# A two-layer attention kernel: the order of the work in which the first layer's loop runs out, and where its norms are split and shifted

## The reference

```python
# first layer, per batch: cross attention on 64 context rows, 16 heads of 16, then an MLP
x = x + (softmax(q k / 4) v) @ Wproj + bproj         # q from layernorm(x), k and v from layernorm(ctx)
h = gelu(layernorm(x) @ W1 + b1)                     # 256 -> 1024
x = x + (h @ W2 + b2)                                # 1024 -> 256
# second layer: self attention (16 heads of 64), cross attention on the context, gated MLP
x = _attn(_ln(x, g1, b1), _ln(x, g1, b1), Wq1, Wk1, Wv1, Wo1, bo1) + x
x = _attn(_ln(x, g2, b2), context, Wq2, Wk2, Wv2, Wo2, bo2) + x
x = _geglu_ff(_ln(x, g3, b3), Wp, bp, Wf, bf) + x
```

## Time and profile before

| what | us |
|---|---|
| median of 3 runs (2285.67 to 2293.39) | 2292.01 |
| the profiled execution | 2292.69 |
| its span in the trace | 2290.9 |
| PE busy in it | 2121.8 (93%) |
| DVE busy | 1608.8 (70%) |
| ACT busy | 1482.3 (65%) |
| GpSimd busy | 1070.5 (47%) |

### The profile page before, as it was taken

One profiled execution on the slowest core, in us unless ns is written; L12 is line 12 of the kernel. 1 busy time (PEld: TensorE's weight loads), 2 busy tenths in 40 slices (PEclk: granted clock), 3 DMA queues, 4 the chain that ended last, 5 costly groups with the idle time before them and its releaser, 6 DMA issues. The chain is left out here.

```text
span 2290.9 us, 31305 instructions
## 1 busy us (share of the span) xinstructions
PE 2121.8 (93%) x11628; PEld 1771.6 (77%) x11628; DVE 1608.8 (70%) x2345; ACT 1482.3 (65%) x2154; POOL 1070.5 (47%) x819
## 2 busy tenths in 40 slices
PE   6868999988899999999999999999997799999998
PEld 4657888876687778777777777777776689888987
DVE  5576767753787787777877778778776766666553
ACT  5546888754777777777777777777774355554431
POOL 2154544441354454454544545545454665656432
PEclk8989999998999999999999999999999999999999
DMA  6810000010000100001001000010004411111000
GB/s 212 297 43 5 22 22 22 20 66 33 19 24 16 37 15 24 24 15 34 15 15 34 15 29 24 15 33 15 24 26 165 138 44 53 56 56 47 10 10 19
DMA packets 84280, 102.67 MB, mean 45 GB/s; under 512 B 29664, under 2 KB 61152, under 8 KB 83616
## 3 DMA queue, kind: packets, MB, share of 16 engines
q1 hardware_dynamic: 84128, 100.66, 13.3%
HBM read 65.50 MB, written 33.82 MB: 43 GB/s over the span
## 5 line engine op out<-in xcount | busy, mean ns | idle before, releaser
L146 PE MATMUL PS<-R 128*128 128x512 f32 (+1 forms) x2944 | 1026.4, 349 | 77.1 <-DVE R L162 46.1
L148 PE MATMUL PS<-R 128*128 128x512 f32 (+1 forms) x2944 | 996.5, 338 | 0.0
L147 PE MATMUL PS<-R 128*128 128x512 f32 (+1 forms) x2944 | 995.8, 338 | 0.0
L146 PEld LDWEIGHTS PS<-R 128*128 128x128 f32 x2944 | 565.8, 192 | 189.9 <-DVE R L162 55.3
L156 ACT ACTIVATE R<-PS 64x512 fp32r<-64x512 f32 (+4 forms) x860 | 460.1, 548 | 239.7 <-PE PS L1805 129.4
L148 PEld LDWEIGHTS PS<-R 128*128 128x128 f32 x2944 | 565.1, 192 | 60.4
L147 PEld LDWEIGHTS PS<-R 128*128 128x128 f32 x2944 | 566.9, 193 | 54.4
L162 DVE TENSOR_TENSOR R<-F,R 128x1024 fp32r<-128x1024 f32 (+2 forms) x416 | 465.2, 1123 | 44.2 <-ACT R L156 22.4
L159 POOL TENSOR_SCALAR R<-F 128x1024 fp32r<-128x1024 f32 (+1 forms) x295 | 266.2, 904 | 284.0 <-DVE F L1958 149.3
L1500 ACT ACTIVATE F<-PS 128x1024 f32<-128x1024 f32 x256 | 263.1, 1028 | 170.3 <-DVE R L162 115.1
L159 POOL TENSOR_SCALAR R<-R 64x512 fp32r<-64x512 f32 x128 | 142.8, 1129 | 391.4 <-ACT R L156 391.4
(11 more groups left out here) (89 smaller groups left out, 1990.9 us busy)
## 6 DMA issues: line engine op xcount, KB each, us to landing
F<-sd SPq DMA_DIRECT2D x128, 128.0 KB, 2.8
xs<-F SPq DMA_DIRECT2D x16, 512.0 KB, 2.6
F<-xs SPq DMA_DIRECT2D x16, 512.0 KB, 3.6
gd<-F SPq DMA_DIRECT2D x8, 768.0 KB, 3.6
vd<-F SPq DMA_DIRECT2D x8, 768.0 KB, 5.9
R<-gd SPq DMA_DIRECT2D x6, 1024.0 KB, 5.5
R<-vd SPq DMA_DIRECT2D x6, 1024.0 KB, 5.7
F<-in_x SPq DMA_DIRECT2D x8, 512.0 KB, 5.7
```

Source lines behind the costliest of these rows:

```text
L146: nc.tensor.matmul(o, L[0], Rr[0], start=start, stop=False, skip_group_check=share)
L147: nc.tensor.matmul(o, L[0], Rr[1], start=False, stop=False, skip_group_check=share)
L148: return nc.tensor.matmul(o, L[1], Rr[0], start=False, stop=stop, skip_group_check=share)
```

## The change

Five parts:

1. From i = 34 (`tail0`) DVE takes the rest of slice n-1 early in iteration i, and of n behind the norm's work, both one iteration sooner than before and ahead of the weight tiles' rests. At i = 41 it also takes the rest of the last slice.
2. The two norms at i = 34 and 36 are split by ACT (hi, 128x1024) and DVE (rest) in place of GpSimd, and DVE adds their bias to x.
3. shift is computed by GpSimd (a product of 128x4) right behind rstd, in all 17 norms of this kind; DVE writes -mean (`less`, 128x4) ahead of it. `less` makes region F 4 words (16 bytes) longer, and all tiles behind it start at other addresses.
4. ACT takes one weight tile in the middle of an iteration and one at its end (before, both at the end). A one-element Exp after the last gelu loads Exp's table ahead of unit 0.
5. Unit 0: the third piece of `next(ahead)` stands at i = 42, ahead of down(63) on PE, ahead of the last `res` on DVE; the last `largest` and the transposes come earlier, and `project_v(0)`, `value(0)` go into the next step (s = 0, behind the k projection of unit 1). The rests of the last four `g3` tiles stand behind that piece on DVE.

The core of the diff:

```diff
             if negated:
+                nc.vector.tensor_scalar(less, mv[:, :, 0], -1.0, None, ALU.mult)
...
-            nc.vector.scalar_tensor_tensor(out=shift, in0=mv[:, :, 0], scalar=-1.0, in1=rstd, op0=ALU.mult, op1=ALU.mult
+            nc.gpsimd.tensor_tensor(shift, less, rstd, ALU.mult).then_inc(ln_shift.sem, 1)
...
-        first1 = (N0 + 7, N0 + 8, N0 + 9, N0 + 11)
+        first1 = (N0 + 7, N0 + 8, N0 + 9, N0 + 10)
+        tail0 = N0 + 2
...
# PE, loop0
+                if i == first1[-1]:
+                    next(ahead)
                 if ok(n - 1, NM):
                     down(n - 1)
...
# ACT, loop0
+                for job in next_weights_at(i)[:1]:
+                    next_weight(job)
...
+                    if i >= tail0:
+                        act.wait_ge(ln_aff, 2 * k + 1)
+                        act.wait_ge(*norm0_free(kind, b))
+                        act_copy(norm0_to(kind, b)[0], xf).then_inc(ln_nh.sem, 1)
...
+                for job in next_weights_at(i)[1:]:
+                    next_weight(job)
                 if i == N0 + LAG0:
+                    nc.scalar.activation(mx4[:, 0:1], prm[:, 0:1], ACT.Exp)
...
# DVE, loop0
-                if ok(n - 2, NM):
+                if ok(n - 2, NM) and i <= tail0:
                     rests(n - 2)
+                if ok(n, NM) and i >= tail0:
+                    rests(n - 1)
...
-                if ok(n - 1, NM):
+                if ok(n - 1, NM) and i < tail0:
                     rests(n - 1)
...
+                if i - 1 in norm0 and i > tail0:
...
+                    nc.vector.tensor_tensor(xv, xv, (brow1 if kind == "g" else brow).unsqueeze(1).to_broadcast([128, 4, C]),
+                                            ALU.add).then_inc(x_bias.sem, 1)
+                if ok(n, NM) and i >= tail0:
+                    rests(n)
+                if i in norm0 and i >= tail0:
...
+                    dve_rest(norm0_to(kind, b)[1], xf, norm0_to(kind, b)[0]).then_inc(ln_nl.sem, 1)
                 for job in next_weights_at(i):
                     dve_weight_rest(job)
+                if n + 2 == NM:
+                    rests(n + 1)
+                if i in first1:
+                    next(ahead)
                 if i == N0 + LAG0:
                     for job in g3[8:]:
                         dve_weight_rest(job)
-                if i in first1:
-                    next(ahead)
...
# GpSimd, loop0
                     ln_pool_rstd(norm0[i + 1][2])
+                    ln_pool_shift(norm0[i + 1][2])
...
-                if i in norm0:
+                if i in norm0 and i < tail0:
...
# PE, second layer (project_v also leaves its old place behind the transposes)
+                    if s == 0 and j == 0:
+                        project_v(0)
...
+                    if u == 0 and j == 3:
+                        yield s
```

More of the change, by code:

```diff
@@ L20 @@
 K_ID, NCON = 0, 128
-NR, NF, NALL = 20480, 3616, 29064
+NR, NF, NALL = 20480, 3620, 29064
 def constants():
@@ L173, in build @@
         mx4, sm4, rc4 = fa.take(16), fa.take(16), [fa.take(16) for _ in range(2)]
-        shift = fa.take(4)
+        shift, less = fa.take(4), fa.take(4)
         xt = fa.take(4, C)
@@ L232, in sp_bias, with ln_stats @@
             nc.sync.dma_start(brow, bias[i].partition_broadcast(128)).then_inc(bias_in.sem, 16)
-        def ln_stats(src, n):
+        def ln_stats(src, n, negated=False):
             dve.wait_ge(par_in, 1)
@@ L245, in ln_stats, with ln_x_stats @@
             dve.wait_ge(dve_step, dve_step.next())
+            if negated:
+                nc.vector.tensor_scalar(less, mv[:, :, 0], -1.0, None, ALU.mult)
             nc.vector.tensor_scalar(ve, mv[:, :, 1], EPS, None, ALU.add).then_inc(ln_var.sem, 1)
-        def ln_x_stats(st, b):
+        def ln_x_stats(st, b, negated=False):
             dve.wait_ge(x_in[x_at(st, b)], load_no[st, b])
-            ln_stats(xbuf(st, b), C)
+            ln_stats(xbuf(st, b), C, negated)
         def ln_pool_rstd(k):
@@ L653, in dve_products @@
             keys5(1)
-            ln_shift_dve(1)
             for job in g0[16:]:
@@ L741, in norm0_bank, with norm0_free @@
             return 6 if i < LAG0 else 0
-        first1 = (N0 + 7, N0 + 8, N0 + 9, N0 + 11)
+        first1 = (N0 + 7, N0 + 8, N0 + 9, N0 + 10)
+        tail0 = N0 + 2
         def norm0_to(kind, b):
             return ns1[b % 2] if kind == "g" else ns[b % 2]
+        def norm0_free(kind, b):
+            if kind == "g":
+                return up_mm, 8 * (b - 2) + 7
+            return q0_mm, 2 * (b - 2) + 1 if kind == "x" else 2 * NB - 3
         def weights0_at(i):
@@ L966, in rounds, with next_weight @@
                 act_copy(h1[n % 3][0], hf1[n % 3]).then_inc(h_hi.sem, 1)
+            def next_weight(job):
+                act.wait_ge(sc0_mm, N0 - 1)
+                act.wait_ge(o0_mm, 2 * NB - 1)
+                act_weight(job)
             act.wait_ge(g5_mm, 15)
@@ L1116, in dve_attention0 @@
                         dve.wait_ge(o0_add, 2 * b + 1)
-                        ln_stats(X1[b % 5], C)
+                        ln_stats(X1[b % 5], C, True)
                     else:
-                        ln_x_stats(norm0_at[kind][0], b)
+                        ln_x_stats(norm0_at[kind][0], b, True)
                 if i % 4 == 2 and ok((i - 2) // 4, NB) and i > 2:
                     value((i - 2) // 4)
+                if i - 1 in norm0 and i > tail0:
+                    kind, b, k = norm0[i - 1]
+                    dve.wait_ge(bias_in, {"g": 1, "s": 2}[kind])
+                    dve.wait_ge(x_bias, k - 2)
+                    xv = xbuf(norm0_at[kind][0], b)
+                    nc.vector.tensor_tensor(xv, xv, (brow1 if kind == "g" else brow).unsqueeze(1).to_broadcast([128, 4, C]),
[3 more added lines that the diff above has]
+                if i in norm0 and i >= tail0:
+                    kind, b, k = norm0[i]
+                    dve.wait_ge(ln_nh, k)
+                    dve_rest(norm0_to(kind, b)[1], xf, norm0_to(kind, b)[0]).then_inc(ln_nl.sem, 1)
                 for job in next_weights_at(i):
                     dve_weight_rest(job)
+                if n + 2 == NM:
+                    rests(n + 1)
+                if i in first1:
+                    next(ahead)
                 if i == N0 + LAG0:
@@ L1156, in pool_attention0 @@
                     divided(i - 1)
-                if i in norm0:
+                if i in norm0 and i < tail0:
                     kind, b, k = norm0[i]
[L1159 to L1162, removed]
+                    pool.wait_ge(*norm0_free(kind, b))
                     ln_split_pool(k, norm0_to(kind, b))
-                if i - 1 in norm0:
+                if i - 1 in norm0 and i <= tail0:
                     kind, b, k = norm0[i - 1]
-                    pool.wait_ge(bias_in, {"x": 0, "g": 1, "s": 2}[kind])
+                    pool.wait_ge(bias_in, {"x": 0, "g": 1}[kind])
                     xv = xbuf(norm0_at[kind][0], b)
@@ L1528, in act_attention1 @@
                         project_k(u)
+                    if s == 0 and j == 1:
+                        value(0)
                     if ok(u, N3) and u > 0 and j == 1:
```

20 lines of the change are left out of this document (4 added, 16 removed).

## The result

The changed kernel takes 2266.67 us (median of 4 runs, 2261.82 to 2267.34) against 2292.7 before in the same comparison: a ratio of 0.9884, interval 0.987 to 0.9898. It is faster by 26 us, as forecast (2267).

The account below looks back on a forecast made before the run. The prediction took TensorE's drain waits for VectorE's late rests as the bound; 15.5 + 2.3 + 6.3 = 24.1 by terms, 26.4 by layout, taken as 25 off 2292.69, then 0.7 for the median, gave 2267 us, range 2259 to 2281.

Parts of the forecast that it names:

- What bounds: Drain between loop and units: TensorE waits 22.2 us, 17.9 of them for rests that VectorE makes late.
- Waits for rests, 15.5: Drain: with needed rests first and norms off GpSimd, waits of 2.8 replace 17.9 + 0.4, saving 15.5 us.
- Unit 0, 2.3: Unit 0's beginning: earlier last maximum and early Exp table load leave waits of 1.6 for 3.9, saving 2.3 us.
- The clock, 6.3: Drain: granted clock returns from 0.90 to 1.00, giving back 6.3 us on 62.85 us of busy time.
- its terms (24.1): Whole gain by sum: 15.5 for waits, 2.3 for unit 0 and 6.3 for the clock make 24.1 us.
- its layout (26.4): TensorE's blocks laid end to end in the new order, without the ends of matmuls: ends 26.4 us earlier.
- The shift, 0: All 17 norms: GpSimd's product taken as 0.4 us; effect on time 0, range -4 to +5.9.
- The addresses, 0: Tiles behind the 16 bytes longer F: no time counted; two `res` at different starts both take 1.28 to 1.29.
- rival C: Second layer's 64 units: moved addresses make operations slower; at 0.6 us per unit, time 2305; chance 0.06.
- o1 weights, 0: o1 loads after the drain: 5.5 of 10.0 us eaten, 4.5 left for the transfer; cost 0, range loss 2.
- Rival A: Drain near i = 36: ScalarE or VectorE falls behind, two waits of about 2.5 return; time 2276; chance 0.16.
- Rival B: All 17 norms: GpSimd's shift takes 1.47, ScalarE's scale waits, eating 22 of 25 us; time 2289; chance 0.08.

Follow-up runs that it names:

- shift_vector: The changed kernel with the shift of all 17 norms on VectorE again, addresses unmoved: 2271.69 us, ratio 0.9914 to the kernel before.
- rests_late: The changed kernel with VectorE's rests of h back in their old order behind the weight tiles' rests: 2280.64 us, ratio 0.9959 to the kernel before.
- gap3: The changed kernel with three idle reductions on VectorE at i = 40, making one wait in the drain: 2273.18 us, ratio 0.992 to the kernel before.
- shift_alone: The kernel before with only the shift moved to GpSimd, -mean written in place so no address moves: 2285.54 us, ratio 0.9978.
- norms_gpsimd: The changed kernel with the norms at i = 34 and 36 split and bias-added on GpSimd again: 2269.7 us, ratio 0.991 to the kernel before.

## Why the prediction was right, point by point

*What bounds.* Right: the drain's waits fell from 22.2 to 4.0, and the drain gave 26.1 us, as much as the median. That the median hit the forecast to 0.3 us is luck: in the later comparison the same kernel, with the same drain (90.78), stood 5 us higher. Its trace there is 5.9 longer, 2.5 of it ahead of the first scores and 4.1 behind the drain, while its start is 0.7 shorter.

*Waits for rests, 15.5.* Right in size: in place of 17.9 + 0.4 stand 1.5 + 1.1. Of the waits that were to stay, 0.4 and 0.4 to 0.6 behind gelus are rows of 0.3 to 0.4, and the 1.1 ahead of the batch's first `down` is 1.18. There the step had the wrong releaser: it is `res` itself, not the rest behind it. Attribution by edit: the order of the rests is worth 11.1 of the drain when it is taken back and 13.7 when it comes alone, unit 0 with the table 5.5, the norms 2.0, the shift 0.1 when taken back and 4.0 when alone. Taken back one by one they sum to 18.7 of 26.1, so the parts overlap.

*Unit 0, 2.3.* Right by the change's own waits (3.9 became 1.4). Undone, it costs more, 5.5, because its wait is longer behind the new order (3.5 in place of 2.0) and brings the lower clock with it.

*The clock, 6.3.* The level came back to 1.00 as said. The term was 1.6 too small: over the whole drain 18.2 of the 26.1 us are idle time and 7.9 are busy time (92.50 became 84.62). The prediction took a clock that is an average over idle and busy time for the busy time alone. It put the 2.3 us between its terms (24.1) and its layout (26.4) down to the ends of matmuls; of the 2.0 that the terms lacked, the rows give 1.6 to the clock. The layout came close, but its blocks stand in no row here.

*The shift, 0.* The price was right in kind (0.24, nearer to the lower end as I took it). The effect was not: the start is 1.9 to 2.6 us shorter in the changed kernel, on the side that my range had as -4. shift_vector shows that it hangs on the shift: 90.40 with VectorE's product (644 ns on average), 87.2 to 87.9 without. That this product had been on the path is not shown: TensorE's idle time is the same with and without it in that pair (24.4 and 24.2), and what differs is its busy time.

*The addresses, 0.* Wrong by 2 us, and not where rival C had looked. The row that I gave against it (two `res` of 1.28 and 1.29) speaks of VectorE, and VectorE indeed did not care; the stores out of the moved tiles took longer. The two misses nearly cancel, about 2 us won at the start and 2 lost ahead of it, which is luck too.

*o1 weights, 0.* Right, with less room than worked out: the loads are issued at 547.96 and ScalarE takes the first tile at 550.54, 2.58 later and without a gap, where I had left 4.5.

*Rival A* did not show: no wait from i = 36 to the loop's end was over 1.18, at the clock's full level. *Rival B* did not: the full swing is 257.55 in place of 257.87.

## What to carry to other kernels

Where an engine waits in a stretch in which no engine is busy, look at the order in which the releasing engine works first: putting the needed result ahead of work that nobody waits for yet gave half of this gain, and left 2 us of drain to the slowness of a neighbour. Lay the waiting engine's blocks end to end in the new order and add the clock's loss behind long waits; here that gave 24.1 by terms and 26.4 by layout, where the drain lost 26.1. Split such a stretch into TensorE's idle and busy time: where the matmuls are the same, a change of the busy time goes with the granted clock and is no part of the waits. When a tile grows by a few words, compare the start addresses of everything behind it, and the DMAs that read there.

## What the runs showed of the hardware that was not expected

A 32-byte shift of the tiles behind F left VectorE's and ScalarE's rows alone and came with stores of 1 KB rows that are 6.4 to 6.8 us long in place of 5.8 to 6.1; stores of 2 KB rows kept their length by the median.

The clock's loss does not follow from a wait's length alone: of two like waits in rests_late one had 0.60 behind it (2.64 us) and one 1.00 (2.59), one of 2.65 in gap3 left the clock at 1.00, one of 6.04 brought 0.50; and nearly the same chain of waits left 0.93 over the drain before and 0.95 in shift_alone. The seven steps of units behind the drain took 34.4 to 36.5 us. TensorE is idle for 6.5 us there both in the changed kernel and in norms_gpsimd, at a clock of 0.95 and 0.86; in the changed kernel's second trace, again at 0.95, it is idle for 7.7. Which of these a run gets was not settled.
